# Casting the last 264 columns of each adjacency row block on GpSimd instead of VectorE

## What is computed

```python
def L0(input, A, h0, y):            # layer 0
    adj = A * (y @ y.T)
    adj = adj / maximum(sum(abs(adj), axis=1), 1e-12)
    return 0.9 * (adj @ input) + 0.1 * h0

def L1(h, adj, simlar, W_proj, b_proj, W_gcn, b_gcn):   # layer 1, simlar = adj
    filt = tanh(adj * simlar) * (adj > 0)
    new_adj = filt kept at its 350 largest entries of each row
    h2 = tanh(h @ W_proj + b_proj)
    return relu(new_adj @ (h2 @ W_gcn) + b_gcn)

x = layernorm(x + L0(x, adj, h0, y))
x = layernorm(x + L1(x, adj, adj, ...))
```

## Time and profile before

| | us |
|---|---|
| median of three runs (465.55 to 465.87) | 465.63 |
| the profiled execution | 466.39 |
| its span in the trace | 464.6 |

### The profile page before, as it was taken

How to read it: one execution, slowest core, us unless ns; L and a number is a source line. 1 busy time by engine, 2 the same in 40 slices (tenths; PEclk the granted TensorE clock), 3 DMA queues, 4 the chain that set the end, 5 groups by cost and what they waited for, 6 DMA issues and landing times.

```text
span 464.6 us, 15132 instructions
## 1 busy us (share of the span) xinstructions
PE 435.6 (94%) x5104; PEld 386.2 (83%) x5104; DVE 378.2 (81%) x1360; ACT 264.0 (57%) x355; POOL 160.1 (34%) x310
## 2 busy tenths in 40 slices
PE   3659999999999999999999999999999999999994
PEld 2447998888889888888888887888888888888883
DVE  5988999999999999999999975766666666666562
ACT  4997999999999999999999943900000000000000
POOL 3012542554444555444455541212212212212222
PEclk9987999999999999999999999999999999999998
DMA  7999999999999999999999300000000000000000
GB/s 260 410 415 422 397 405 421 413 415 412 416 419 418 422 424 426 414 416 419 420 423 415 104 3 1 13 11 17 11 17 17 12 16 17 17 11 17 17 11 23
DMA packets 25518, 108.50 MB, mean 234 GB/s; under 512 B 5097, under 2 KB 15490, under 8 KB 15490
## 3 DMA queue, kind: packets, MB, share of 16 engines
q1 hardware_dynamic: 25490, 108.14, 57.8%
HBM read 105.57 MB, written 2.56 MB: 233 GB/s over the span
## 4 chain that ended last, share of the span: by engine, by line
PE 75%; DVE 10%; issue 5%; ACT 5%; DMA 2%; POOL 2%; POOLq 0%; DVEq 0%; ACTq 0%; SPq 0%
PE acc L528 63%; PE words L476 6%; DVE a_bits L790 3%; DMA a_rows<-in_adj_dram 2%; PE feat_acc L591 2%; PE proj_acc L602 2%; ACT count_out L692 2%; DVE turned L877 2%; PE xnt_acc L583 1%; ACT count_out L685 1%; ACT x_parts L671 1%; ACT count_out L762 1%; POOL xs L443 1%; DVE z_high L932 1%; ACT count_out L753 1%
## 5 line engine op out<-in xcount | busy, mean ns | idle before, releaser
L528 PE MATMUL acc<-x_parts,turned 128*128 128x257 f16 (+1 forms) x1600 | 193.2, 277 | 4.6 <-DVE turned L877 3.5
L685 ACT ACTIVATE count_out<-a_rows,ones 128x2688 bf16<-128x2688 f32 (+1 forms) x80 | 190.1, 2377 | 0.7 <-DMA a_rows<-in_adj_dram 0.3
L528 PEld LDWEIGHTS acc<-x_parts,turned 128*128 128x128 fp8e4 (+1 forms) x1600 | 155.2, 99 | 28.0 <-issue 5.2
L528 PE MATMUL acc<-f_parts,turned 128*128 128x256 f16 (+1 forms) x1560 | 169.6, 271 | 0.8 <-DVE turned L877 0.8
L528 PEld LDWEIGHTS acc<-f_parts,turned 128*128 128x128 fp8e4 (+1 forms) x1560 | 150.6, 98 | 18.8 <-issue 1.2
L790 DVE TENSOR_SCALAR a_bits<-a_rows 128x2688 bf16<-128x2688 f32 (+1 forms) x80 | 116.6, 1457 | 2.6 <-DMA a_rows<-in_adj_dram 2.2
L426 POOL TENSOR_TENSOR var_eps<-mean_var,consts 128x1 f32<-128x1 f32 x80 | 18.6, 232 | 266.2 <-DVE mean_var L1092 137.9
L877 DVE TENSOR_SCALAR turned<-a_words 128x320 uint16 (+1 forms) x305 | 66.5, 232 | 51.2 <-PE acc L528 50.9
L429 POOL TENSOR_TENSOR rstd<-var_eps,consts 128x1 f32<-128x1 f32 x80 | 87.5, 1094 | 6.3
L877 DVE TENSOR_SCALAR turned<-same_class 128x320 uint16<-128x320 uint16 x313 | 71.3, 253 | 0.1
L476 PEld LDWEIGHTS words<-pack,a_bits 128*128 128x128 bf16 (+1 forms) x1600 | 51.6, 97 | 9.7 <-DVE a_bits L790 7.8
(11 more groups left out here) (112 smaller groups left out, 288.4 us busy)
## 6 DMA issues: line engine op xcount, KB each, us to landing
a_rows<-in_adj_dram SPq DMA_DIRECT2D x39, 1344.0 KB, 7.5
a_rows<-in_adj_dram SPq DMA_DIRECT2D x39, 1156.0 KB, 8.0
out_dram<-xn SPq DMA_DIRECT2D x39, 64.0 KB, 1.5
h_rows<-in_L_gnn_h_dram SPq DMA_DIRECT2D x19, 128.0 KB, 7.7
xs<-in_x_dram SPq DMA_DIRECT2D x3, 640.0 KB, 10.0
xs<-in_x_dram SPq DMA_DIRECT2D x1, 512.0 KB, 9.0
y_nat<-in_L_gnn_y_dram SPq DMA_DIRECT2D x1, 304.0 KB, 3.6
a_rows<-in_adj_dram SPq DMA_DIRECT2D x1, 84.0 KB
```

The lines of the kernel that those rows point to most:

```text
L528: mm = pe.matmul(acc[par][0:m, used], bits, parts[:, b, used], start=first and b == blocks[0], stop=last and b == blocks[-1])
L685: act.activation(count_out[0:m, 0:w], a_rows[par][h][0:m, 0:w], ACT.Relu, bias=ones[0:m, 0:1], scale=-HUGE, accum_out=col).then_inc(s_coun ...
```

## The change

The last three column blocks of half 1 (b = 37, 38 and 39: 2048 to 2312 of the half, 4736 to 5000 of the row, 264 columns) are cast by GpSimd. VectorE's cast of half 1 stops at column 2048 of the half. GpSimd's new instruction stands between `residual` and `inverse_std` of its step, and waits for the rows of half 1 and for the packing of half 1 of the block before. TensorE waits for it (`s_edge`) before it packs column block 37, and SyncE's load of half 1 waits for it too. GpSimd's wait for `x` moves from ahead of its steps to its first `residual`, so that its first casts don't wait for it.

```diff
+    EDGE = (NB - 3) * P - HB * P
 ...
                         sp.wait_ge(s_counted, t * 2 - 3 + h)
+                        if h == 1:
+                            sp.wait_ge(s_edge, t * 2 - 3 + h)
 ...
             def residual(n, par, i, c):
                 m = rows_of(n)
+                if isinstance(n, int) and n == 0:
+                    for q in range(4):
+                        pool.wait_ge(s_in[f"x{q}"], 16 if q else 32)
+                    pool.wait_ge(s_in["xt"], 16)
 ...
+            def cast_edge(t, par, pair):
+                m = rows_of(t)
+                w = HALF[1].stop - HALF[1].start
+                pool.wait_ge(s_rows[par][1], pair * 16 + 16)
+                if not isinstance(t, int) or t >= 1:
+                    pool.wait_ge(s_packed, t * 2)
+                pool.sem_inc(s_passed, 1)
+                pool.tensor_scalar(a_bits[1][0:m, EDGE:w], a_rows[par][1][0:m, EDGE:w], 1.0, None,
+                                   ALU.is_equal).then_inc(s_edge, 2)
 ...
                 if valid(t - 2):
                     residual(t - 2, par, i, c - 2)
+                if valid(t):
+                    cast_edge(t, par, pair)
                 if valid(t - 3):
                     inverse_std(t - 3, odd, rows_of(t - 3))
 ...
-            for q in range(4):
-                pool.wait_ge(s_in[f"x{q}"], 16 if q else 32)
-            pool.wait_ge(s_in["xt"], 16)
+            pool.wait_ge(s_cleared, 2)
 ...
                 for b in range(h * HB, HB if h == 0 else NB):
+                    if b == NB - 3:
+                        pe.wait_ge(s_edge, t * 2 + 2)
 ...
             def cast(t, par, pair, h):
                 m = rows_of(t)
-                w = HALF[h].stop - HALF[h].start
+                w = EDGE if h == 1 else HALF[h].stop - HALF[h].start
```

More of the change, by code:

```diff
@@ L257, in packed_path @@
         s_counted = sem("s_counted")
+        s_edge = sem("s_edge")
         s_packed = sem("s_packed")
```

## The result

The changed kernel takes 467.0 us (median of 10 runs) against 465.78 (median of 10) for the one before, run beside it: a ratio of 1.0028, 95% interval 1.0020 to 1.0036. It is slower by 1.2 us, clear of the noise, but not by the 12.5 of the forecast. The profiled execution took 467.01 us, its span 465.2.

What follows compares the result with a forecast made beforehand. VectorE was taken to set the first stage's pace, TensorE right behind. Delay 0.49 less saving 0.144 gave +0.35 us a step, over 36 steps +12.5 us: 478.9, or 478.1 for the median; 8-in-10 range 463.5 to 492.

Steps and rivals of the forecast that it cites:

- the floor below it: First stage: rival that VectorE isn't held up and the saving is cut at TensorE's 6.14 us a step; 462.0, chance 0.19.
- the delay of VectorE by GpSimd's cast: First-stage steps: GpSimd's new cast delays VectorE by 0.49 us a step, the mean of two cases, 0.60 and 0.38.
- for as long as it lasts: First stage: a GpSimd instruction on SBUF holds up VectorE's unpacks, casts and normalizing for its whole duration, taken as 0.65 us.
- GpSimd keeps the port from `xh` on: At VectorE's unpack waiting for `xh`: the new cast follows directly, so that unpack waits longer, about 0.60 us of delay.
- The second did: Behind `xh`: VectorE slips its waiting unpack in before the new cast; delay 0.27 or 0.50 us, mean 0.38.
- No change: Rival: a 0.40 us GpSimd cast with VectorE slipping in between delays it 0.14 us, eating the saving; 465.6, chance 0.09.
- The second floor: First-stage row loads: the transfer becomes a floor at about 6.21 us a step once the stored-up lead is used.
- The +5 us: First stage: sum if GpSimd's one-input cast is roughly line-rate, at the low end of 0.40 us, rather than about +12.

Runs made afterwards that it cites:

- the series: Changed kernel plus, behind its end, six stretches of 40 unpack-like VectorE instructions beside GpSimd instructions of one kind each; 516.11 us in one execution, only its trace used.
- e2: Changed kernel, but VectorE casts all 2312 columns of half 1 and GpSimd casts the last 264 besides, into a scratch buffer; 472.63 us, ratio 1.0147.
- e3: Changed kernel with GpSimd's tensor_scalar replaced by a tensor_tensor of the same 264 columns; 471.78 us, ratio 1.0129.
- e5: Changed kernel without GpSimd's cast, last 264 columns taken as zero, packed-words verdict left out, output not right; 462.25 us, ratio 0.9917.
- e6: Changed kernel with GpSimd's tensor_scalar replaced by a copy of the same 264 columns; 465.09 us, ratio 0.9977.
- e8: Changed kernel with GpSimd's cast made a copy and started only when VectorE's third unpack of the step is done; 462.68 us, ratio 0.9923.
- e7: Changed kernel with one wait more: GpSimd's cast starts only when VectorE's third unpack of the step is done; 463.0 us, ratio 0.9932.

## Why the prediction was wrong

The direction was right, and so was the place: GpSimd's cast starts where `xh` ends, it holds up the unpacks, `z_high` and `z` keep their 0.34, TensorE doesn't wait before column block 37, SyncE and `inverse_std` are not delayed. VectorE set the pace, and the time at the floor below it was priced rightly (462.0, measured 462.25). The failing step is one term, the delay of VectorE by GpSimd's cast: 0.49 us a step in the sum, 0.165 measured. With it the net is 0.165 - 0.138 = 0.03 us a step and the sum 36 x 0.03 = +1.0 us, where +1.2 was measured.

- *The duration was taken for the hold.* The step "for as long as it lasts" rested on `xh` and `h_part`, which end nearly together with VectorE's instruction that waits for them. But an instruction of GpSimd holds VectorE only for part of its duration: 0.21 of 0.40 us in the series' tensor_tensor of 128 columns, 0.40 of 0.87 in the new one. The unpack at 197.79 began 0.05 us after `xh` and ended 0.11 after it, but it lost only 0.52 - 0.22 = 0.30 us, beside an `xh` of 0.46. So that row puts the hold of `xh` between 0.30 and 0.46, and the prediction took the upper end; of another kind of instruction it says nothing. It could be told, for each kind, by counting how many of VectorE's instructions get through beside one of GpSimd's.
- *Two errors of the size went opposite ways.* The duration was 0.89 us, not 0.65. Had the sum been made with the right duration, it would have been worse: 0.73 x 36 less the saving, +21 us.
- *Two cases, averaged.* The first, "GpSimd keeps the port from `xh` on", did not occur: no unpack from 100 to 220 us takes more than 0.53, and the one that meets `xh` keeps its 0.52 or 0.43. The second did, with a delay of 0.22 or 0 us where the prediction had 0.50 or 0.27.
- *No change* was one of the rivals, with "the saving is eaten exactly" at a delay of 0.14 us. That is what happened within 0.03 us a step, but by another way: the rival got there by a duration of 0.40, the chip by a hold shorter than its 0.89. It had a chance of 0.09, and its nearness is luck.
- *The second floor.* The transfer was put at 6.21 us a step; three kernels run below that (6.159 to 6.188), so it was too high by 0.02 to 0.05. The forecast's sum did not use it.

By the Trainium skill, SBUF — State Buffer, section Who interferes with whom, the blocking lasts for the whole instruction, and the prediction said that the durations agree. They don't settle it, and the run with the series shows otherwise here, as far as the trace's durations go: VectorE starts two to four instructions for each one of GpSimd's, and loses less than its duration. By the Trainium skill, GPSIMD Engine Reference, section 4.1 Engine selection, one-input work is roughly line-rate. The tensor_scalar is not: 0.87 us for 264 columns against 0.53 for 128 is 2.5 ns a column, where VectorE's cast takes 0.545. The copy is nearer, (0.41 - 0.29) / 136 = 0.9 ns a column. The +5 us that the prediction worked out from that page is nearer to the measured +1.2 than its own sum, but by a duration of 0.40 that was 0.89.

Of the rest of the sum: in the trace after, the first steps were ahead by 1.0 us at block 4 and 0.3 at block 8. Whether that comes from the moved wait for `x` or from the arrival of the first loads wasn't tried. All the other kernels have the moved wait too; those of e2, e3, e5, e6 and e8 were ahead by 1.0 to 1.2 us at block 4, that of e7 was 1.1 behind.

## What to carry to other kernels

Here the price of moving work from VectorE to GpSimd wasn't GpSimd's duration but the part of it in which VectorE couldn't run its SBUF work, and this depended on what VectorE did at that moment. So first find a stretch in which VectorE reads PSUM or has one long instruction of its own, and start GpSimd's instruction there with a wait: the same cast cost 1.2 us where it fell and gained 3.1 us a little later. And where a row shows two instructions ending together, read also how much longer than usual the held one took: that, and not the other's duration, is what was lost.

## What the runs showed of the hardware

Not expected: that the longer of two GpSimd instructions over the same 264 columns (0.87 against 0.63 us) held VectorE up less in the kernel, beside a hold that in the series comes in two pieces of about 0.2 us half a microsecond apart; that the hold grows with the columns and differs by kind (0.7 to 0.8 ns a column for a copy, 1.3 to 1.6 for the others, from two sizes each) while 0.2 us or more of each instruction's duration hold nothing (0.47 of the 0.87); and that in e7_later GpSimd's instruction, caught by VectorE's cast of 1.21 us, took 1.87 us without costing VectorE anything.
